# Two cross-attentions: row maxima by pairs of banks, key copies on another engine or in another place, and the root of the variance between GpSimd's two products

## The reference

```
first:   logits = q k^T / 4 + (1 - mask) * -1e9
         attn   = softmax(logits) * group_prob          # group_prob is per sequence, query, key
second:  attn   = softmax(q k^T / 4)
both:    x = x + (attn v) Wo + bo,    k = ctx Wk + bk,  v = ctx Wv + bv
```

## Time and profile before

| | |
|---|---|
| median of 3 runs | 1037.44 us (1036.21 to 1040.33) |
| the profiled execution | 1034.94 us, of it 1033.1 us span |
| first cross-attention | from about 18 to about 190 us of the span |
| second cross-attention | from about 389 to about 545 us |
| TensorE busy | 786.5 us (76%) |
| VectorE, ScalarE, GpSimd busy | 519.6, 440.8, 437.2 us |

### The profile page before, as it was taken

The page is one execution under the profiler, slowest core; times in us unless marked ns, Lnnn a source line. Parts: engine busy times, 40 slices in busy tenths (PEclk is TensorE's granted clock), DMA queues, the critical chain, the costliest instruction groups (busy, mean ns, idle before and its releaser), DMA issues.

```text
span 1033.1 us, 21352 instructions
## 1 busy us (share of the span) xinstructions
PE 786.5 (76%) x7200; PEld 571.0 (55%) x7200; DVE 519.6 (50%) x1397; ACT 440.8 (43%) x1523; POOL 437.2 (42%) x637
## 2 busy tenths in 40 slices
PE   2788987699779566999975626765555999999980
PEld 1676766588644235777754415654432566666660
DVE  3466766467733344667665765666231333223323
ACT  1667667246514225777751023766102333333320
POOL 4566654434468768687722334354341000000005
PEclk9999999889879888999996756886556999999995
DMA  8322214723331545454410003122292065152004
GB/s 285 137 67 79 70 53 143 240 73 95 123 124 54 190 133 170 147 172 136 155 51 0 0 0 122 43 83 97 92 391 77 27 223 179 49 189 93 16 23 122
DMA packets 66199, 116.83 MB, mean 113 GB/s; under 512 B 6576, under 2 KB 22704, under 8 KB 65456
## 3 DMA queue, kind: packets, MB, share of 16 engines
q1 hardware_dynamic: 57936, 105.25, 30.3%
q10 hardware_dynamic: 6624, 6.03, 1.8%
q0 software_dynamic: 1536, 4.20, 1.3%
HBM read 81.11 MB, written 34.34 MB: 112 GB/s over the span
## 4 chain that ended last, share of the span: by engine, by line
PE 48%; DVE 15%; POOL 13%; ACT 9%; issue 8%; DMA 4%; ACTq 0%; SPq 0%; DVEq 0%; POOLq 0%; another core or an unknown queue 0%
ACT probs L1208 6%; PE ps L622 4%; PE ps L1046 4%; PE ps L1047 4%; PE ps L1048 4%; PE ps L638 3%; PE ps L1069 2%; PE ps L1071 2%; PE ps L1070 2%; PE ps L1058 2%; PE ps L520 2%; DVE probs L1710 2%; POOL probs L1454 2%; PE ps L662 2%; PE ps L521 2%
## 5 line engine op out<-in xcount | busy, mean ns | idle before, releaser
L1393 POOL TENSOR_TENSOR piece_out<-piece_in,piece_out 128x512 f16<-128x512 f32 x96 | 116.6, 1215 | 7.7
L1609 POOL DMA_INDIRECT pt<-y_rows,neg x16 | 15.4, 960 | 233.4 <-DMA y_rows<-vbuf 228.8
L2133 DVE TENSOR_TENSOR probs<-ps,ctx_t 128x512 f32<-128x512 f32 x46 | 29.6, 686 | 154.0 <-PE ps L1048 154.0
L622 PE MATMUL ps<-pack_const,probs 128*128 128x128 f32 x512 | 74.3, 278 | 17.0 <-issue 13.1
L1358 POOL TENSOR_TENSOR var<-mv,half 128x1 f32<-128x1 f32 x48 | 9.6, 199 | 179.4 <-DVE mv L1625 107.7
L622 PEld LDWEIGHTS ps<-pack_const,probs 128*128 128x128 f32 x512 | 55.9, 140 | 37.7 <-issue 26.0
L1392 POOL CAST piece_out<-piece_in 128x512 f16<-128x512 f32 x96 | 62.2, 648 | 23.0 <-DMA piece_in<-in_w 22.1
L1046 PE MATMUL ps<-arena,qbuf 128*128 x184 | 70.7, 384 | 0.0
L1047 PE MATMUL ps<-arena,qbuf 128*128 x184 | 70.5, 383 | 0.0
L1048 PE MATMUL ps<-arena,qbuf 128*128 x184 | 70.3, 382 | 0.0
L1158 ACT ACTIVATE probs<-ps,mx 128x256 f32<-128x256 f32 x128 | 59.2, 487 | 15.6 <-DVE mx L1721 15.6
(11 more groups left out here) (285 smaller groups left out, 2178.5 us busy)
## 6 DMA issues: line engine op xcount, KB each, us to landing
piece_in<-in_w SPq DMA_DIRECT2D x96, 256.0 KB, 2.8
w_parts<-piece_out SPq DMA_DIRECT2D x96, 256.0 KB, 2.1
arena<-w_parts SPq DMA_DIRECT2D x8, 3072.0 KB, 12.7
ctx_t<-in_ctx SPq DMA_DIRECT2D x32, 256.0 KB, 2.8
x_rows<-piece_out SPq DMA_DIRECT2D x1, 2944.0 KB, 17.3
qbuf<-x_rows ACTq DMA_DIRECT2D x23, 128.0 KB, 2.4
y_rows<-vbuf ACTq DMA_DIRECT2D x23, 128.0 KB, 1.9
arena<-in_xa SPq DMA_DIRECT2D x2, 1282.0 KB, 7.8
```

The lines of the kernel that those rows point to most:

```text
L622: last = pe.transpose(AB[:, o:o + P], pr[:, 2 * c + n, kt * P:(kt + 1) * P], ident)
L1393: pool.tensor_tensor(both[:, PIECE:], src, both[:, 0:PIECE], ALU.subtract).then_inc(piece_split, 1)
```

## The change

In the first cross-attention ScalarE does four exponentials, then copies the keys, then does the other four; GpSimd takes the root of the variance between the two products in place of behind them; `add_bias` moves from even to odd steps. In the second the two row maxima go over banks 0 and 1 and over banks 2 and 3, the exponentials go in `PAIR_ORDER`, four behind each maximum, and the keys are copied by VectorE (bias added in one instruction of 128x512) between the divided outputs and the normalised rows; ScalarE no longer copies keys there. TensorE's waits for the exponentials follow the new order. `add_bias` moves in the second as well.

```diff
@@ TensorE, turn_probs
-                            hold(pe, g["weighted"], 4 * b + c + 1)
+                            hold(pe, g["weighted"], 4 * b + (1, 3, 2, 4)[c])
@@ ScalarE
-                def exps(b, s):
-                    for i, n in enumerate(PAIR_ORDER):
+                def exps(b, s, first):
+                    for i, n in list(enumerate(PAIR_ORDER))[first:first + 4]:
                         hold(act, g["masked"], 8 * b + i + 1)
...
-                def plain_exps(b, s, pairs):
-
-                    hold(act, g["maxima"], 2 * b + 2)
-                    for n in pairs:
+                def plain_exps(b, s):
+
+                    for i, n in enumerate(PAIR_ORDER):
+                        if i % 4 == 0:
+                            hold(act, g["maxima"], 2 * b + i // 4 + 1)
...
                     if live(k, 2, SEQS):
                         if st == "xa0":
-                            exps(k - 2, k % 2)
+                            exps(k - 2, k % 2, 0)
                         else:
-                            plain_exps(k - 2, k % 2, pairs[:4])
-                    if live(k, 0, SEQS):
+                            plain_exps(k - 2, k % 2)
+                    if live(k, 0, SEQS) and st == "xa0":
                         copy_keys(k, k % 2)
+                    if live(k, 2, SEQS) and st == "xa0":
+                        exps(k - 2, k % 2, 4)
                     if k % 2 == 1 and live(k, 1, SEQS) and st == "xa0":
                         copy_queries(k // 2)
-                    if live(k, 2, SEQS) and st == "xa1":
-                        plain_exps(k - 2, k % 2, pairs[4:])
@@ GpSimd
-                def weigh(b, s):
-                    for c in (0, 2):
+                def weigh(b, s, chunks):
+                    for c in chunks:
...
-                    if k % 2 == 0 and live(k, 0, SEQS):
+                    if k % 2 == 1 and live(k, 1, SEQS):
                         hold(pool, prev["normed"], h + 1)
                         add_bias(g, h, w["bo"], prev["resid"] if st == "xa1" else prev["normed"])
                     if live(k, 2, SEQS) and st == "xa0":
-                        weigh(k - 2, k % 2)
+                        weigh(k - 2, k % 2, (0,))
                     if k % 2 == 0 and live(k, 6, SEQS):
                         root_of_variance(g, h - 3)
+                    if live(k, 2, SEQS) and st == "xa0":
+                        weigh(k - 2, k % 2, (2,))
@@ VectorE
-                    banks = S.rearrange("p (j f k) -> p f j k", j=4, f=2)
+                    banks = S.rearrange("p (j f k) -> p j f k", j=4, f=2)
+                    largest = mx[:, s * HEADS:s * HEADS + PAIRS].rearrange("p (f j) -> p j f", f=2)
                     hold(dve, g["scored"], b + 1)
-                    for hf in range(2):
-                        dve.tensor_reduce(mx[:, s * HEADS + 4 * hf:s * HEADS + 4 * hf + 4], banks[:, hf, :, :],
+                    for two_banks in (slice(0, 2), slice(2, 4)):
+                        dve.tensor_reduce(largest[:, two_banks, :], banks[:, two_banks, :, :],
                                           AX.X, ALU.max, negate=True).then_inc(g["maxima"].sem, 1)
+
+                def copy_keys(b, s):
+                    hold(dve, g["k_projected"], b + 1)
+                    dve.tensor_tensor(k32[:, s * 512:(s + 1) * 512].rearrange("p (f n) -> p f n", f=2),
+                                      AB[:, 0:512].rearrange("p (f n) -> p f n", f=2),
+                                      w["bk"].unsqueeze(2).broadcast_to([P, 2, KEYS]), ALU.add)\
+                       .then_inc(g["k_copied"].sem, 1)
...
                         normalise_outputs(k - 4, k % 2, h - 2)
+                    if live(k, 0, SEQS) and st == "xa1":
+                        copy_keys(k, k % 2)
                     if k % 2 == 0 and live(k, 6, SEQS):
```

More of the change, by code:

```diff
@@ L1164, in step @@
                 def step(k):
-                    pairs = range(PAIRS)
                     if live(k, 2, SEQS):
                         if st == "xa0":
-                            exps(k - 2, k % 2)
+                            exps(k - 2, k % 2, 0)
                         else:
-                            plain_exps(k - 2, k % 2, pairs[:4])
-                    if live(k, 0, SEQS):
+                            plain_exps(k - 2, k % 2)
+                    if live(k, 0, SEQS) and st == "xa0":
                         copy_keys(k, k % 2)
+                    if live(k, 2, SEQS) and st == "xa0":
+                        exps(k - 2, k % 2, 4)
                     if k % 2 == 1 and live(k, 1, SEQS) and st == "xa0":
                         copy_queries(k // 2)
-                    if live(k, 2, SEQS) and st == "xa1":
-                        plain_exps(k - 2, k % 2, pairs[4:])
                     if live(k, 3, SEQS):
```

## The result

The changed kernel takes 1027.47 us (median of 5 runs, 1024.92 to 1029.41) beside 1036.21 for the kernel before on the same chip (5 runs): ratio 0.9916, 95% interval 0.9897 to 0.9935. It is faster by 8.7 us, where 18.9 were forecast. The profiled execution took 1029.01 us (span 1027.2), 1.5 above that median.

A forecast was written before the change was run, and what follows sets the result against it. No single engine bounds the kernel; chains of waits across four engines do, read interval by interval. Gains of 12.0 us (first attention) and 6.9 (second), 18.9 together, take the median from 1037.44 to 1018.5 us, range 1012 to 1029.

The forecast's parts named there:

- I add 0.15, bounds 0 and 0.26: First attention, even intervals: normalised rows beside GpSimd's second product take 0.15 us longer, leaving a gain of 1.11 each.
- the earlier root was to give 0.4: First attention, k = 16: no keys there, so the earlier root alone gains 0.4 us.
- The normalised rows behind it move from 5.75 to 6.21: Second attention, even intervals: VectorE's key copy delays the normalised rows from 5.75 to 6.21 us into the interval.
- forecast loss of 0.16: Second attention, even intervals: chunk 3 moves from 7.86 to 8.02, losing 0.16 us each, five times 0.8.
- lies beside other work: First attention, odd intervals: GpSimd's added `add_bias` of 0.69 us delays nothing, as its products are wanted later.
- turned rows that still wait 0.9: Sign that the prediction is wrong: turned rows still idle 0.9 us, having idled 0.89 for VectorE in the first's even interval.
- nameless waits: TensorE's "issue" waits before chunk 2's transposes, 0.77 us in the first's odd interval, are waits for ScalarE's key copy.
- slower: Rival, chance 0.08: ScalarE, stopped at `copy_keys` until TensorE has projected, becomes the bound; 5.7 us slower, 1043.1.
- hidden anyway: Rival, chance 0.10: "issue" waits aren't key copies, chunk 2 moves nowhere; gain 4 us, 1033.4.
- the second scores: Second attention's start, k = 2: scores that waited 3.38 us for exponentials come 1.75 earlier, wait below 2.
- Half of it: Rival, chance 0.25: an unseen wait replaces one chain in the first, half the second's gain remains; gain 10 us, 1027.4.
- GpSimd's root still arrives late (contention, statistics): Clause of the rival with chance 0.25: a late root in the first attention's even intervals loses 5.5 us of gain.

The follow-up runs named there:

- experiment 4: Changed kernel with GpSimd waiting for the normalised rows in both attentions and the first tile's bias back in step 0: 1011.51 us, 0.9783 of the kernel before.
- experiment 1: Changed kernel, but in even steps of both attentions GpSimd waits behind the root until the normalised rows are done: 1014.49 us, 0.9786 of the kernel before.
- after_again: The changed kernel unaltered, run again beside the kernels with either attention's part alone: 1026.26 us, 0.9902 of the kernel before.

## Why the prediction was wrong

- **The failed step** is the term "I add 0.15, bounds 0 and 0.26" in the first's even intervals. It measured 0.86 (1.28 for 0.42). I had read the durations of the earlier trace rows as one price that other traffic makes larger, and so took the difference of two medians. The runs showed a stop in its place: the rows last until GpSimd's instruction beside them ends, plus 0.15, or 0.41 where none runs. They were short before because a short instruction happened to stand there: a mask of 0.40, a cast of 0.61. The change put a product of 1.27 there. With 0.86 in place of 0.15 the sum gives 1.11 - 0.71 = 0.40 gained, and 0.41 was measured. At k = 16, where the earlier root was to give 0.4, the same stop made it a loss of 0.4.
- **The same in the second attention, not counted at all.** "The normalised rows behind it move from 5.75 to 6.21" was right (6.23), but by this they left the cast of 0.61 us for the subtraction of 1.16, and 0.57 became 1.33: five times 0.76 on top of the forecast loss of 0.16, together the 0.92 measured. The stops are 3.5 (first, even), 0.8 (k = 16) and 3.8 (second, even) of the 10.1 us missing.
- **The bias "lies beside other work"** holds in the steady state and not in step 1, where it delays the first mask by 0.7, the larger part of the 1.1 us missing at the start (experiment 4). The prediction's sign of being wrong, turned rows that still wait 0.9, came true with 0.89.
- **Right:** the nameless waits were the key copies (chunk 2 starts without idle time in odd intervals, and in the even ones too); ScalarE idles 0.31 and 1.29 us for the keys (0.4 and 1.4 forecast) and nobody waits for it, so "slower" and "hidden anyway" are out; the root ends 6.26 into the interval (6.25 forecast), and GpSimd's second product at 7.49 (7.5); row maxima by pairs of banks cost the same 1.22; the key copy on VectorE is hidden in odd intervals; the second scores wait 1.53 instead of 3.38. "Half of it" gave 1027.4, and 1027.47 was measured, but that is luck: its clause "GpSimd's root still arrives late (contention, statistics)" did not come true. The root was punctual, its reader was stopped, and the second attention lost 4.6 of its 6.9 us, 3.8 of them by a stop that this rival didn't have.
- With the stop taken away (experiment 1) the rest of the working holds: 8.28 and 8.78 in the first, where it gives 8.27 and, without the 0.15, 8.79; 7.80 and 8.64 in the second, where it gives 7.82 and 8.79. The last is 0.15 better because the rows take 0.40 there and no longer 0.57. The gain was 21 us.

## What to carry to other kernels

An engine's instruction that is longer in one place than in another is a question about its neighbour: compare its end with the ends on the other engines before averaging durations into a price. Before moving GpSimd work, look at which VectorE instructions from SBUF to SBUF will start during it; if one of them is on the path, let a short GpSimd instruction stand there, or make GpSimd wait, which here lengthened no interval and turned about 9 us of gain into 21. And an edit that makes a value earlier (the root) can make its reader later, so follow the chain to the reader's end.

## What the runs showed of the hardware

- A VectorE `tensor_scalar` with one float32 tensor input and its output in SBUF (128x256, 0.41 us alone) that comes second doesn't finish until the GpSimd instruction beside it has ended, whether that has one input (0.40, 0.61 us) or two (0.64, 1.16, 1.27, 2.35 us); it ends 0.14 to 0.16 us after it, and between two GpSimd instructions in a row it gets through. The Trainium skill (SBUF — State Buffer, Who interferes with whom) says this as a rule for VectorE instructions in a 2-port mode, which `tensor_scalar` can enter: whoever issues first holds a pair of ports that the two engines share for its whole instruction, and the other "fully blocks". The durations here agree, though no trace shows the mode. It is a stronger statement than the "contends" that the prediction cited: with the forecast's own times (second product until 7.5) and the 0.15, the rows would end at 7.65, and they ended at 7.64.
- It goes the other way as well. In four traces, later in the program, the rows come first: they take their 0.41, and GpSimd's product of 0.73 takes 0.89 or 0.90. The rows, then the product, in `after_again`:

```profile
562.32 0.41 DVE L1631 TENSOR_SCALAR xn_all<-x,mv,rstd  x1 [1.07 <-POOL rstd L1359]
...
562.42 0.89 POOL L1585 TENSOR_TENSOR junk<-xn_all,arena 128x256 f32<-128x256 f32 x1 [0.28 <-issue]
```

- The start in the record doesn't tell which of the two comes first: at 448.88 the rows are recorded 0.03 us ahead of the subtraction (448.91) that stopped them. In the changed kernel's trace the rows at 564.11 are 0.11 us ahead of the same product as above (564.22, 0.73) and take 0.98, ending 0.14 behind it.
- VectorE's instructions that read PSUM run at their usual length beside the same GpSimd work: 0.59 for two of L1669 beside a mask, 0.67 to 0.69 for L1729 and L1676 beside casts and subtractions.
